# Second and output products with hi and lo weights side by side: 512-column moving operands, four y banks, one score bank and one shared bank

## The reference

```python
xn = _layernorm(x)
x = x + attention(xn, Wqkv, Wout) + relu(xn @ W1 + b1) @ W2 + b2
```

## Time and profile before

| | us |
|---|---|
| median of 3 runs | 1140.32 |
| lowest and highest run | 1138.23, 1140.84 |
| the profiled execution's own time | 1139.81 |
| its span, first to last instruction | 1138.0 |
| VectorE busy | 745.6 (66%) |
| ScalarE busy | 651.5 (57%) |
| GpSimd busy | 619.0 (54%) |

### The profile page before, as it was taken

How to read it: one execution, slowest core, us unless ns; L and a number is a source line. 1 busy time by engine, 2 the same in 40 slices (tenths; PEclk the granted TensorE clock), 3 DMA queues, 4 the chain that set the end, 5 groups by cost and what they waited for, 6 DMA issues and landing times.

```text
span 1138.0 us, 23173 instructions
## 1 busy us (share of the span) xinstructions
PE 1109.6 (97%) x7457; PEld 939.7 (83%) x7457; DVE 745.6 (66%) x1370; ACT 651.5 (57%) x1078; POOL 619.0 (54%) x488
## 2 busy tenths in 40 slices
PE   5799999999999999999999999999999999999997
PEld 4478988888888888888888888888888888888886
DVE  7777667667666757666667666667666667677540
ACT  4546556556556556555655555655565565555652
POOL 2435555555555555565565556565466465565464
PEclk9999999999999999999999999999999999999999
DMA  6445454444444444445344544444445343544421
GB/s 188 102 116 128 118 130 113 104 114 117 124 125 111 108 107 124 119 115 126 96 119 111 132 109 122 108 111 118 126 102 137 91 126 106 138 100 110 102 76 60
DMA packets 96139, 130.57 MB, mean 115 GB/s; under 512 B 25840, under 2 KB 54128, under 8 KB 96112
## 3 DMA queue, kind: packets, MB, share of 16 engines
q1 hardware_dynamic: 96112, 130.23, 44.8%
HBM read 39.98 MB, written 18.87 MB: 52 GB/s over the span
## 4 chain that ended last, share of the span: by engine, by line
PE 95%; DVE 2%; issue 1%; POOL 1%; POOLq 0%; ACT 0%; DVEq 0%
PE y_bank L738 40%; PE h_bank L738 39%; PE misc L872 6%; PE s_bank L800 5%; PE misc L813 2%; PE misc L738 2%; DVE xn L620 0%; DVE w_exp L635 0%; DVE s_max L629 0%; PE misc L838 0%; PE misc L821 0%; DVE xn_keys L590 0%; DVE w_lo L554 0%; PE s_bank L738 0%; POOL att L394 0%
## 5 line engine op out<-in xcount | busy, mean ns | idle before, releaser
L387 POOL TENSOR_TENSOR h_lo<-h_full,h_hi 128x512 fp32r<-128x512 f32 x256 | 335.7, 1313 | 464.2 <-ACT h_full L453 460.1
L459 ACT ACTIVATE w_exp<-w_exp 128x512 f32<-128x512 f32 x256 | 162.7, 636 | 237.6 <-DVE w_exp L635 237.4
L738 PE MATMUL y_bank<-w_hi,h_hi 128*128 128x256 f32 x1024 | 290.0, 283 | 0.0
L738 PE MATMUL y_bank<-w_lo,h_hi 128*128 128x256 f32 x1024 | 289.8, 283 | 0.0
L738 PE MATMUL y_bank<-w_hi,h_lo 128*128 128x256 f32 x1024 | 289.5, 283 | 0.0
L451 ACT ACTIVATE h_hi<-h_bank,b_cols 128x512 fp32r<-128x512 f32 x256 | 175.8, 687 | 106.5 <-PE h_bank L738 100.9
L629 DVE TENSOR_REDUCE s_max<-s_bank 128x8 f32<-128x512 f32 x256 | 175.4, 685 | 69.8 <-PE s_bank L800 68.0
L738 PE MATMUL h_bank<-xt_hi,w_hi 128*128 128x512 f32 x512 | 211.2, 413 | 2.4 <-DVE q_lo L658 2.4
L738 PEld LDWEIGHTS y_bank<-w_lo,h_hi 128*128 128x128 f32 x1024 | 195.3, 191 | 9.8
L738 PEld LDWEIGHTS y_bank<-w_hi,h_hi 128*128 128x128 f32 x1024 | 194.8, 190 | 9.2
L738 PE MATMUL h_bank<-xt_hi,w_lo 128*128 128x512 f32 x512 | 202.2, 395 | 0.0
(11 more groups left out here) (87 smaller groups left out, 1606.9 us busy)
## 6 DMA issues: line engine op xcount, KB each, us to landing
q_pack<-q_hi SPq DMA_DIRECT2D x256, 128.0 KB, 2.4
x_raw<-x SPq DMA_DIRECT2D x32, 512.0 KB, 3.4
q_pack<-q_lo SPq DMA_DIRECT2D x128, 128.0 KB, 2.4
rden_rows<-rden_dram SPq DMA_DIRECT2D x128, 128.0 KB, 3.5
out<-y SPq DMA_DIRECT2D x32, 512.0 KB, 2.9
k_pack<-k_hi SPq DMA_DIRECT2D x256, 32.0 KB, 1.9
num_den<-num_den SPq DMA_DIRECT2D x32, 256.0 KB, 2.5
k_pack<-k_lo SPq DMA_DIRECT2D x128, 32.0 KB, 1.9
```

The lines of the kernel that those rows point to most:

```text
L387: pool.tensor_tensor(h_part[1][:, i % HBUF], h_full[:, i % HBUF], f32(h_part[0][:, i % HBUF]), ALU.subtract).then_inc(h_lo, 1)
L459: act.activation(w_exp[:, pair], w_exp[:, pair], ACT.Exp).then_inc(w_ready, 1)
L738: mm = pe.matmul(ps, stationary[a], moving[b], start=start and c == 0 and n == 0, stop=stop and c == len(pairs) - 1 and n == 2, skip_group ...
```

## The change

The hi and lo weights of the second product and of the output product are stored side by side, and a new `wide_products` replaces `three_products` there. It issues one matmul with the stationary hi part and both weight parts (512 columns, into the two halves of a bank) and one with the stationary lo part and the hi weights (256 columns, into the first half). Each of the four tiles has a whole y bank; VectorE adds its two halves in two operations. The PSUM left is two h banks, one score bank and one misc bank. Score n waits for the shift of pair n-1; the weighted values use misc and the score bank, so they wait for the shift of pair 7, and the next step's score 0 for their drain; the two halves of the transposes go through misc one after the other, and the key work through misc alone. The orders on TensorE, ScalarE and VectorE are rewritten for this: hidden block i ahead of the exponential of pair i-3, normalise in two halves after pairs 1 and 2, the key operations earlier, the last second product ahead of the queries. In step -2 the y banks stand in for misc.

```diff
-        wout = [sb(f"wout_{n}", [P, DH, D], F32R) for n in ("hi", "lo")]
+        wout_parts = sb("wout_parts", [P, DH, 2, D], F32R)
+        wout = [wout_parts[:, :, n] for n in range(2)]
...
-        misc = [misc_banks[:, i] for i in range(2)]
+        pv_banks = ctx.enter_context(nc.psum_tensor("pv_banks", [P, 2, SEG], F32))
+        misc, s_bank = pv_banks[:, 0], pv_banks[:, 1]
...
-        s_bank = [bank(f"s_bank{i}") for i in range(2)]
-        y_bank = [bank(f"y_bank{i}") for i in range(YB)]
+        y_banks = ctx.enter_context(nc.psum_tensor("y_banks", [P, T, PIECES, D], F32))
...
             def step(s, par, ffn, attention, norm, load):
-                for i in range(LAG, NH - 1):
+                for i in range(LAG, NH):
+                    if attention and i > LAG:
+                        exponential(s, i - LAG - 1)
+                    if i in first:
+                        hidden(past(s), first[i])
                     if i == 3 and norm and par == 0:
                         keys_hi(s)
-                    if attention:
-                        exponential(s, i - LAG)
-                    if i in first:
-                        hidden(past(s), first[i])
-                if norm:
-                    transposed_hi(s, par)
-                if NH - 1 in first:
-                    hidden(s, NH - 1)
+                if norm:
+                    transposed_hi(s, par, 0)
                 if attention:
                     exponential(s, PAIRS - 3)
+                if norm:
+                    transposed_hi(s, par, 1)
...
                 for n in range(PAIRS):
+                    if attention:
+                        shift_scores(s, n)
                     if n == 0 and keys:
                         normalise_keys(s + 2)
-                    if n == 4 and keys:
-                        drain_kv(s)
-                    if n == 5 and keys:
-                        mask_k(s)
-                    if n == 6 and norm:
-                        transposed_lo(s, par)
-                    if attention:
-                        shift_scores(s, n)
-                    if n == 1 and norm:
-                        normalise(s + 2, par)
                     if n == 1 and keys:
                         keys_lo(s)
-                    if n == 4 and ffn:
+                    if n in (1, 2) and norm:
+                        normalise(s + 2, par, n - 1)
+                    if n == 2 and keys:
+                        drain_kv(s)
+                    if n == 3 and keys:
+                        mask_k(s)
+                    if n == 3 and ffn:
                         invert_den(s)
+                    if n in (5, 6) and norm:
+                        transposed_lo(s, par, n - 5)
...
-                        dve.tensor_tensor(y[:, par, 2 * b:2 * b + 2],
-                                          y_bank[b][:].rearrange("p (t d) -> p t d", t=2),
-                                          x_b2[:, par, 2 * b:2 * b + 2], ALU.add).then_inc(y_ready, 1)
+                        dve.tensor_tensor(y[:, par, rows], y_banks[:, rows, 0], x_b2[:, par, rows], ALU.add).then_inc(y_half, 1)
+                        dve.wait_ge(y_half, s * YB + b + 1)
+                        dve.tensor_tensor(y[:, par, rows], y_banks[:, rows, 1], y[:, par, rows], ALU.add).then_inc(y_ready, 1)
...
+            def wide_products(t, stationary, moving, start, stop):
+
+                pe.matmul(y_banks[:, t].rearrange("p a d -> p (a d)"), stationary[0],
+                          moving.rearrange("p a d -> p (a d)"), start=start, stop=False, skip_group_check=True)
+                return pe.matmul(y_banks[:, t, 0], stationary[1], moving[:, 0], start=False, stop=stop,
+                                 skip_group_check=True)
...
-                    mm = three_products(y_bank[t // 2][:, (t % 2) * D:(t % 2 + 1) * D],
-                                        [([h[:, i % HBUF, t * P:(t + 1) * P] for h in h_part],
-                                          [w[:, i, :] for w in w2s])], i == 0 and t % 2 == 0, False, alone=False)
+                    mm = wide_products(t, [h[:, i % HBUF, t * P:(t + 1) * P] for h in h_part], w2_parts[:, i],
+                                       i == 0, False)
...
-                pe.wait_ge(s_shifted, past((s + 1) * PAIRS + n - 1))
-                pe.matmul(s_bank[n % 2][:], k_pack[0:PR, pair], q_pack[0:PR, pair], start=True,
+                if n == 0:
+                    pe.wait_ge(num_den_ready, past((s + 1) * QUADS))
+                pe.wait_ge(s_shifted, past((s + 1) * PAIRS + n))
+                pe.matmul(s_bank, k_pack[0:PR, pair], q_pack[0:PR, pair], start=True,
...
                 for i in range(LAG, NH):
-                    if i == 3 and norm and par == 0:
-                        transpose_keys(s)
-                    if i == 5 and norm and par == 0:
-                        keys_values(s)
-                    if i == 6 and norm and par == 0:
-                        transpose_k(s)
-                    if i == NH - 1 and norm:
-                        transpose_x(s, par)
+                    if attention and i > LAG:
+                        scores(s, i - LAG)
                     if i in first:
                         first_product(past(s), first[i], par if ffn else 1 - par)
-                    if attention and i > LAG:
-                        scores(s, i - 1)
+                    if norm and par == 0:
+                        if i == 3:
+                            transpose_keys(s)
+                        if i == 4:
+                            keys_values(s)
+                        if i == 5:
+                            transpose_k(s)
+                    if i == NH - 1 and norm:
+                        transpose_x(s, par, 0)
                     if i in second:
                         second_product(past(s), second[i])
+                if attention:
+                    scores(s, PAIRS - 2)
                 if ffn:
                     second_product(s, NH - 2)
-                if attention:
-                    scores(s, NH - 1)
-                if norm:
-                    for m in range(DH):
-                        queries(s, par, m)
+                if norm:
+                    transpose_x(s, par, 1)
+                if attention:
+                    scores(s, PAIRS - 1)
                 if ffn:
-                    second_product(s, NH - 1, range(T - 1))
+                    second_product(s, NH - 1)
+                if norm:
+                    queries(s, par, 0)
+                    queries(s, par, 1, range(DH - 1))
                 if attention:
                     weighted_values_waits(s, 0, norm)
-                if ffn:
-                    second_product(s, NH - 1, range(T - 1, T))
+                if norm:
+                    queries(s, par, 1, range(DH - 1, DH))
```

144 lines of the change are left out of this document (79 added, 65 removed).

## The result

| | before | after |
|---|---|---|
| median (lowest to highest) | 1140.32 (1138.23 to 1140.99) | 1163.11 (1162.18 to 1164.01) |
| profiled execution's own time | 1139.81 | 1162.18 |
| its span | 1138.0 | 1159.2 |
| ratio of medians, 95% interval | | 1.0201 (1.0187 to 1.0215) |

The changed kernel is slower by 22.8 us at the median, where I had forecast 12 and had put the upper end of the range at 1162. The sign and most of the mechanism hold; one term, "Filling", does not. Further runs of the changed kernel, unedited (experiment 14), gave 1.0195.

The account below looks back on a forecast made before the run. TensorE was taken as the bound, its matmuls covering 1109.6 of 1138 us. Terms -9.5 + 2.6 + 0.7 + 3.4 + 10.2 + 3.1 + 2 = +12.5 gave 1152.5 us, with an 8 in 10 range of 1134 to 1162.

Parts of the forecast that it names:

- Filling: Steps -1 and 0: uncovered score round trips +3.0, first shift no longer behind key normalisation -1.3; +2, bounds 0 and +4.
- The port collision: Odd steps: GpSimd's residual and h_lo hold up normalise, so score 3 waits 0.68, in 15 steps +10.2 us.
- Rivals 1 and 2: Odd-step score 3 not late: 1137 or 1131, chance 0.27; without better matmul, or half the collisions: 1138 to 1143, chance 0.15.
- rival 3: Even steps lose 0.5 us too, as key normalisation meets h_lo of iteration 2: +7.5, 1160; chance 0.15.
- Odd steps near 34.1, even ones near 35.3: Step lengths in us that the trace would show if the forecast waits at scores were there.
- Wide products: Second and output products: a 512- and a 256-column matmul replace three narrow ones, 0.3525 for 0.360 per triple, -9.5 us.
- Rival 4: Second and output products: no cheaper wide matmul, +9.5, 1162 us; chance 0.05.
- Transposes in two halves: First 512-column matmul behind each of two transpose groups pays 0.085 more, so twice per step: +2.6 us.
- Waits at scores 1 and 7: TensorE waits for VectorE's shift, 0.11 at score 1 (+3.4) and 0.10 at score 7 (+3.1), each 31 times.
- The second addition: VectorE's extra 0.69 operation per half of y: +0.7 at the kernel's end, +3.4 between steps through score 1.

Follow-up runs that it names:

- experiment 14: The changed kernel, unedited, measured once more: 1161.54 us, ratio 1.0195 to the kernel before.
- Experiment 1: Changed kernel with GpSimd's residual behind h_lo of block 4 in place of block 2: 1149.35 us, ratio 1.0076.
- experiment 2: Changed kernel with each wide matmul issued as two of 256 columns, banks, additions and order kept: 1170.02 us, ratio 1.0251.
- experiment 10: Kernel of experiment 9 with each wide matmul issued as two of 256 columns again: 1149.0 us, ratio 1.0084.
- experiment 9: Kernel of Experiment 1 with the matmuls of scores 1 and 7 issued a little later on TensorE: 1139.97 us, ratio 1.0004.
- experiment 6: Kernel of Experiment 1 without the second addition, so the lo weights' products are not added: 1142.5 us, ratio 1.0027.
- 13: Kernel of experiment 9 with a second score bank for every odd pair of step -1: 1139.04 us, ratio 0.9989.
- 16: Kernel of experiment 9 with two score banks in step -1, measured once more: 1141.34 us, ratio 1.0008.
- experiment 4: Kernel before with one score bank in steps -1 and 0 only, in the old order: 1151.6 us, ratio 1.0096.
- 12: Changed kernel with a second score bank for every odd pair of step -1: 1159.48 us, ratio 1.0174.
- 15: Changed kernel with two score banks in step -1, measured once more: 1160.04 us, ratio 1.0176.
- experiment 3: Kernel before with GpSimd's residual behind h_lo of block 4: 1140.4 us, ratio 0.9998.

## Why the prediction was right and wrong

**The port collision: right, nearly to the tenth.** The walk through the odd step, in us from its first score, against the rows at 577.30 and after: residual 4.5 to 6.9 (measured 4.60 to 7.02), normalise issued at 4.9 (4.94), both tiles done at 8.45 (8.48), shift 2 from 8.37 (8.40), score 3 at 9.91 (9.86) with TensorE there at 9.23 (9.24), the second pair done at 11.2 (11.13). The wait was 0.62 for 0.68. (ScalarE's program has the exponential of pair i-3 ahead of hidden block i, so block 2 has none ahead of it, as this walk assumes.) Experiment 1 confirms it: the residual moved, and 0.72 per odd step went. The rule that the prediction took from the Trainium skill ("SBUF — State Buffer", Who interferes with whom), one engine holds the port for its whole instruction and the other is fully blocked, agrees: with the residual elsewhere the tiles took 0.73 for 3.54. Rivals 1 and 2, the collision missed or met in half the steps, are out (all odd steps but the first and the last take 34.11 or 34.14, those two 33.90); so is rival 3, since the even steps lost under 0.1. "Odd steps near 34.1, even ones near 35.3" measured 34.14 and 35.19 to 35.23.

**Wide products: right per matmul, half lost in the steps.** In second products a pair takes 0.350 (0.233 + 0.117, medians) against a triple of 0.359: 0.009 for the 0.0075 predicted. The steady steps have 29 x 40 pairs, for which the prediction's price gives 8.7; they saved 5.2 (experiment 2) or 5.5 (experiment 10), while the medians differ by 6.9 and 9.0. The Trainium skill's gap ("TensorE: Matmul & The Clock Gate", Back-to-back issue gap) gave an estimate of 2.5 ns per triple; the 9 ns in these rows don't agree with it. Rival 4, no cheaper wide matmul, is out.

**Transposes in two halves: right.** In experiment 9, where no wait covers it, the first 512-column matmul behind each of the two groups takes 0.316 and 0.321, where before had 0.321 once.

**Waits at scores 1 and 7: right in place, under-sized.** Score 1 starts at 3.07 for a predicted 3.15, but the matmul behind it starts 0.33 later (580.37 to 580.70), where one behind a score that didn't wait starts 0.24 later (583.48 to 583.72 in the timeline). The prediction counted the wait and not this. Scores 1, 3 and 7 pay it, some 0.1 each.

**The steady steps as a whole.** Between the first scores of steps 1 and 30 the runs take the loss apart, in this order: the collision 10.4 (experiment 1), the waits at scores 1 and 7 7.9 (experiment 9), the wide matmuls -5.5 (experiment 10), and what is left of the new order and the split transposes -1.3 (experiment 10 against before). The sum is the +11.5 measured. The prediction's terms for these 29 steps are 10.2, 6.1, -8.7 and 2.4, together +10.0. So the two errors here are the waits, 1.8 too small, and the wide matmuls, 3.2 too large, and the 3.7 that the new order gained for other reasons, which it didn't look for, took the most of them back.

**The second addition.** 0.8 at the end for 0.7. Without it the steady steps gained 4.2 (experiment 6), where the prediction had 3.4 for its wait at score 1.

**Filling: this is the step that failed.** It had +3.0 for step -1 and -1.3 for step 0, and +2 with bounds of 0 and +4. Measured: +6.4 up to the first score of step 0, +2.4 in step 0, 8.7 together. (Before and after have the same kind of start.) Four errors in it, by the rows of the start:
- The count. I took five scores without cover in both kernels; before had four. The new order, score n one iteration later, adds a whole one.
- The round trip. I took 1.98 for each, which needs a free VectorE and the higher clock. Half of normalise stands ahead of one (2.62), and two have a score matmul at the lower granted clock (2.39 and 2.28). And before had 1.29 on average, not 1.40. With 4 x 2.32 for 3 x 1.29 the +3.0 becomes +5.4: 2.0 for the trip more, 2.1 for the three others at 1.98, 0.6 for normalise and 0.7 for the clock.
- The drain. "The next step's score 0 waits for the drain" stands in the change; I checked the weighted values' wait in a full step and not in step -1, which has no output product. +1.1 between queries and score 0.
- Step 0. The key normalisation in front of shift 0 does go away, but it moved behind it, and with one bank it delays score 2. Experiment 1, where the residual is elsewhere, has step 0 at 32.99, 2.15 less. Of these, the delay itself is 1.5, and 1.0 of it is won back by score 3. The other 1.6 come between scores 6 and 7, where the changed kernel has a second stretch of the lower clock (76.1 to 79.5) and experiment 1 has none. Whether this stretch follows from the delay isn't shown: other profiles have it without the delay (experiments 13 and 16).

Of the +9.9 that the profiled execution had beyond the sum (22.4 for 12.5), Filling is 6.7, the steady steps 1.7 (against the terms for all 31 steps, +9.8), the end 0.2, and 1.2 lies outside the span.

What stays open is how the start divides between one bank, the new order and the shared bank. One bank in the old order cost 11.3 (experiment 4). Giving the second bank back in step -1 of the new order brought 1.3 to 1.5 by step 0 (12, 13 and 15), because the transposes through the one shared bank then hold the queries; no run gave these a second bank as well. The lower granted clock has a share that the rows price only in places (0.7 in the round trips, 1.6 in step 0), and no run changed it alone.

## What to carry to other kernels

By these runs, taking a buffer from a short round trip is safe only where the producer's period exceeds the round trip plus the longest piece of other work that can stand in it, blocked operations included; walk that out once per kind of step, and once more for the pipeline's filling, where there is no other work to hide it. The filling, two of 34 steps, held two fifths of the loss. And an instruction of GpSimd that costs nothing beside two buffers (experiment 3) can cost 0.7 in every odd step beside one (experiment 1): when a buffer goes, look again at what was harmless.

## What the runs showed of the hardware

- A matmul behind a score matmul that had waited starts 0.33 after it, for 0.24 otherwise: a wait costs some 0.1 more than its own length on TensorE (scores 1 and 3 in the rows above).
- A 256-column matmul behind a 512-column one takes 0.117, in a row of its own kind 0.120, and a 512-column one 0.233 (medians over the second products). So merging two saves 6 ns on the pair and 3 on the next matmul. In whole steps less than that arrived (5.5 us for 1160 triples, experiment 10).
- Moving GpSimd's instruction out of VectorE's way took two operations of 256 columns from 3.54 to 0.73, while GpSimd's own duration stayed (2.42 and 2.40). Between the residual and the h_lo that was waiting behind it one of the two operations got through, so they came in turn.
- Where the stretches of the lower granted clock fall varies. In 14 of 18 profiles one falls on the products behind the first score of step -1. Where the order is that of the changed kernel, score 1 then comes at 30.6 to 31.4, otherwise at 28.8 to 29.1. At the end the stretch from the first score of step 30 to the last matmul takes 57.5 in one profile of the changed kernel and 56.2 in the other, whose span is 1.6 shorter.
- The score matmul takes 0.47 to 0.50 behind idle time in the one level and 0.77 to 0.79 in the other, and a round trip through one bank 1.98 and 2.28 to 2.39.
- So an edit of the start that is worth under 2 us can't be judged by first and last times of two profiles. Counted from a common event (here score 1 of step -1), the second bank of step -1 came out as 1.3, 1.5 and 1.5 us in three pairs of profiles.
